# Attention layers of 16 heads worked four heads at a time, and a small attention layer run in another order

## The reference

```python
# causal (first): 16 heads of 8 channels, over the 256 positions of each sequence
scores = q @ k.T / sqrt(8) + triu(-1e8, k=1); out = softmax(scores) @ v; x += out @ Wo.T
# lead (fifth): 16 heads of 8 channels, over the LEADING axis: for each of the 256
# positions, the 8 sequences attend to one another (scores are 8 x 8 for each head)
scores = einsum('sbhd,tbhd->bhst', q, k) / sqrt(8); x += (softmax(scores) @ v) @ W.T
# binary (seventh): as causal without the mask, with weights mean|W| * sign(W) and biases
x += softmax(q @ k.T / sqrt(8)) @ v @ Wp.T + bp
```

## Time and profile before

| | us |
|---|---|
| median of 3 runs (4507.86 to 4510.74) | 4509.04 |
| the profiled execution, time | 4513.09 |
| its span, first to last instruction | 4511.3 |
| causal heads, first projection to last residual | 25.5 to 246.3 |
| lead, first projection to last residual | 3806.4 to 3921.0 |
| binary heads, first projection to last residual | 4104.3 to 4350.5 |
| TensorE busy, share of the span | 89% |

### The profile page before, as it was taken

The page is one execution under the profiler, slowest core; times in us unless marked ns, Lnnn a source line. Parts: engine busy times, 40 slices in busy tenths (PEclk is TensorE's granted clock), DMA queues, the critical chain, the costliest instruction groups (busy, mean ns, idle before and its releaser), DMA issues.

```text
span 4511.3 us, 169577 instructions
## 1 busy us (share of the span) xinstructions
PE 4027.8 (89%) x69543; PEld 2810.5 (62%) x69543; DVE 2763.2 (61%) x4602; ACT 2729.5 (61%) x5657; POOL 3001.0 (67%) x1858
## 2 busy tenths in 40 slices
PE   8979999999999999977999999999999995367975
PEld 5656666666666666635666666666666663154654
DVE  4556666666766667635667666676666663524541
ACT  5656676666766766635667667576675763134652
POOL 0068888888888888816888878788787882421011
PEclk9999999999999999989999999999999997587987
DMA  2023343434334343312334333343333330040004
GB/s 68 2 59 94 101 104 91 108 92 105 100 92 111 90 103 101 96 30 60 94 102 103 94 101 95 101 103 94 101 96 99 102 90 19 0 119 8 1 11 124
DMA packets 349841, 368.13 MB, mean 82 GB/s; under 512 B 58738, under 2 KB 285171, under 8 KB 348787
## 3 DMA queue, kind: packets, MB, share of 16 engines
q1 hardware_dynamic: 338834, 348.79, 30.0%
q0 software_dynamic: 2048, 4.20, 0.3%
q10 hardware_dynamic: 8160, 3.93, 0.3%
HBM read 246.99 MB, written 109.71 MB: 79 GB/s over the span
## 4 chain that ended last, share of the span: by engine, by line
PE 42%; ACT 2%; POOL 2%; DVE 2%; issue 2%; DMA 1%; DVEq 0%; POOLq 0%; ACTq 0%
PE banks L328 7%; PE banks L359 4%; PE banks L407 4%; PE banks L333 3%; PE banks L451 3%; PE banks L312 3%; PE banks L295 2%; PE banks L879 2%; PE banks L377 2%; PE banks L897 1%; PE banks L445 1%; PE banks L914 1%; PE banks L392 1%; PE banks L1345 1%; PE banks L1365 1%
## 5 line engine op out<-in xcount | busy, mean ns | idle before, releaser
L671 POOL TENSOR_TENSOR arena<-arena 128x512 f32<-128x512 f32 x768 | 960.0, 1271 | 461.3 <-DVE arena L600 266.5
L676 POOL TENSOR_TENSOR arena<-arena 128x1024 f32<-128x1024 f32 x384 | 905.9, 2359 | 30.1
L673 POOL TENSOR_TENSOR arena<-arena 128x1024 f32<-128x1024 f32 x384 | 908.1, 2365 | 0.0
L600 DVE SCALAR_TENSOR_TENSOR arena<-arena,banks 128x512 f32<-128x512 f32 x768 | 493.6, 684 | 537.3 <-ACT arena L500 528.7
L328 PE MATMUL banks<-w_qk,arena 128*128 128x512 f32 x1536 | 734.8, 601 | 16.0 <-DVE arena L700 10.6
L461 ACT COPY arena<-banks 128x512 f32<-128x512 f32 x384 | 224.6, 585 | 660.0 <-PE banks L407 660.0
L593 DVE TENSOR_REDUCE arena<-arena 128x8 f32<-128x512 f32 x768 | 494.0, 679 | 83.4 <-ACT arena L477 81.0
L477 ACT ACTIVATE arena<-banks 128x512 f32<-128x512 f32 x768 | 441.7, 594 | 62.0 <-PE banks L328 49.4
L407 PE MATMUL banks<-ident,arena 128*128 128x128 f32 x3072 | 427.1, 282 | 34.9 <-POOL arena L676 22.8
L328 PEld LDWEIGHTS banks<-w_qk,arena 128*128 128x128 f32 x1536 | 277.0, 193 | 272.1 <-issue 272.0
L333 PEld LDWEIGHTS banks<-w_v,arena 128*128 128x128 f32 x1536 | 293.9, 191 | 206.6 <-issue 186.5
(11 more groups left out here) (220 smaller groups left out, 6744.8 us busy)
## 6 DMA issues: line engine op xcount, KB each, us to landing
v_rows<-arena SPq DMA_DIRECT2D x1536, 64.0 KB
arena<-v_rows SPq DMA_DIRECT2D x768, 128.0 KB
arena<-v_rows SPq DMA_DIRECT2D x768, 112.0 KB
arena<-in_moe_w SPq DMA_DIRECT2D x30, 515.5 KB, 3.8
w_qk<-in_stack_qk SPq DMA_DIRECT2D x48, 256.0 KB, 3.0
w_v<-in_stack_v SPq DMA_DIRECT2D x48, 128.0 KB, 3.2
w_o<-in_stack_o SPq DMA_DIRECT2D x12, 512.0 KB
w_w<-in_stack_w SPq DMA_DIRECT2D x12, 341.0 KB, 3.0
```

The costliest lines, as they stand in the source:

```text
L600: last = nc.vector.scalar_tensor_tensor(qn[:, :, tile], rn, 1e12, bank(M, tile).rearrange("p (h q d) -> p h q d", h=GH, q=2), ALU.min, ALU ...
L671: nc.gpsimd.tensor_tensor(f.sined[:, :, :, half, :], x[:, :, :, 1 - half, :], sines[:, :, mine].unsqueeze(1).to_broadcast([D, GH, 4, DH // ...
L673: nc.gpsimd.tensor_tensor(rot, x.rearrange("p h t a d -> p h t (a d)"), cosines.unsqueeze(1).to_broadcast([D, GH, 4, DH]), ALU.mult).then_ ...
L676: nc.gpsimd.tensor_tensor(rot, rot, f.sined.rearrange("p h t a d -> p h t (a d)"), ALU.add).then_inc(S.rotated, 1)
```

## The change

Both head modules go by *quads*: 4 in each sequence, 32 steps, each quad being heads c, 4+c, 8+c and 12+c. The scores of the four heads go to banks 0 to 3, all at once, and the next quad's scores wait until all four heads have been exponentiated. DVE takes the maxima one head and one query tile at a time (8 instructions of 128 or 256 columns for a quad, in place of 2 of 1024) and signals after each head; ACT makes the exponentials of a head as soon as it has its maxima. Turning and copying goes in two halves of two heads. Causal scores and mask are placed so that 384 columns hold all that is computed (the mask covers 2 x 128 columns of each bank). The values of head c lie shifted by 8c rows in their 32, so the outputs of four quads accumulate in bank 6 in natural order: one Ln, Exp, multiply and one output matmul for a sequence, in place of four. TensorE's order in step n is: turn the first half of quad n-1, scores of quad n, outputs of quad n-2, turn the second half of quad n-1, projections. The last binarised weight is turned whole. In lead, buffers are doubled (four products), POOL makes all 16 query products, then all 16 value products; the softmax of t = 0 falls in the query products of t = 1.

```diff
 def pe_heads(M, pe, m):
+    def turn(h, half):
+        pe.wait_ge(S.probs, 2 * h.n + half + 1)
+        if h.n or half:
+            pe.wait_ge(S.copied_first, 2 * h.n + half)
+            pe.wait_ge(S.copied_second, 2 * h.n + half)
+        for i in range(2):
...
+                    last = pe.transpose(bank(M, 4 + i)[:, o:o + 128],
+                                        f.p[:, h.n % 2, 2 * half + i, qt, kt * 128:kt * 128 + 128], M.ident[:])
+        last.then_inc(S.turned, 1)
+    for n in range(QUADS + 3):
+        if 0 <= n - 1 < QUADS:
+            turn(Quad(m, n - 1), 0)
+        if n < QUADS:
+            if n >= 1:
+                pe.wait_ge(S.probs, 2 * n)
             if m.causal:
+                for j in range(4):
+                    pe.matmul(bank(M, j).rearrange("p (t k) -> p t k", t=2)[:, :, 0:128], M.identb[:],
+                              M.cmask[:, 0:2 * 128], start=True, stop=False, skip_group_check=True)
             for t in range(2):
+                for j in range(4):
                     r = slice(32 * j, 32 * j + 32)
+                    last = pe.matmul(bank(M, j)[:, cols], f.qm[r, h.b % 2, h.c, t * 128:t * 128 + 128],
+                                     f.k[r, h.b % 2, 0:cols.stop - cols.start], ...)
             last.then_inc(S.scores, 1)
+        if 0 <= n - 2 < QUADS:
+            h = Quad(m, n - 2)
+            pe.wait_ge(S.copied_first, 2 * h.n + 2)
+            pe.wait_ge(S.copied_second, 2 * h.n + 2)
+            ...  # 16 matmuls into bank 6, start only for c == 0, stop only for c == 3
+        if 0 <= n - 1 < QUADS:
+            turn(Quad(m, n - 1), 1)
+        if n % 4 == 0 and n // 4 + 1 < B:
+            project_qk(n // 4 + 1)
+        if n % 4 == 1 and n // 4 + 1 < B:
+            project_v(n // 4 + 1)
+        if n % 4 == 2 and n >= 6:
+            project_out(n // 4 - 1)
 def act_heads(M, act, m):      # dve_heads: the same order, with maxima in the place of exponentials
+    for n in range(QUADS + 3):
+        if 0 <= n - 1 < QUADS:
+            copy(Quad(m, n - 1), 0)
+        if n < QUADS:
+            exponentials(Quad(m, n), 0)
+        if 0 <= n - 1 < QUADS:
+            copy(Quad(m, n - 1), 1)
+        if n < QUADS:
+            exponentials(Quad(m, n), 1)
 def dve_heads(M, dve, m):
-    nc.vector.memset(f.v.rearrange("p a t h e -> p (a t h e)"), 0.0)
+    nc.vector.memset(f.vs.rearrange("p a g e -> p (a g e)"), 0.0)
+    def maxima(h, half):
+        dve.wait_ge(S.scores, h.n + 1)
+        for j in (2 * half, 2 * half + 1):
+            for t in range(2):
+                last = nc.vector.tensor_reduce(f.ntop[:, h.n % 2, j, t:t + 1], bank(M, j)[:, h.keys[t]], AX.X, ALU.max,
+                                               negate=True)
+            last.then_inc(S.maxed, 1)
 def pool_lead(M, pool, m):
+    for j in range(4 * B):
+        t, s = j // B % 2, j % B
+        if j >= 4:
+            if j - 4 < 2 * B:
+                pool.wait_ge(S.reduced, j - 3)
+            else:
+                pool.wait_ge(S.att, j - 3 - 2 * B)
+        if j < 2 * B:
+            ...  # product of query s with all keys of t
+        else:
+            pool.wait_ge(S.step, 4 * t + 4)
+            ...  # product of the probabilities of query s with all values of t
```

More of the change, by code:

```diff
@@ L957, in act_heads @@
     take_v(0)
[L958 to L984, removed]
-                                                bias=f.ntop[:, n % 2, 2 * i + t:2 * i + t + 1])
-            last.then_inc(S.probs, 1)
-            if h.x == 1 and h.b + 1 < B:
-                take_qk(h.b + 1)
-            if h.x == 3 and h.b + 1 < B:
-                take_v(h.b + 1)
@@ new lines, in copy, with exponentials @@
+    def copy(h, half):
+        act.wait_ge(S.turned, 2 * h.n + half + 1)
+        if h.n >= 2:
+            act.wait_ge(S.pv, h.n - 1)
+        nc.scalar.copy(f.pt[:, h.n % 2, 2 * half, 0:h.width], bank(M, 4, h.width)).then_inc(S.copied_first, 1)
+    def exponentials(h, half):
+        if h.n >= 2:
+            act.wait_ge(S.turned, 2 * h.n - 2)
+        for j in (2 * half, 2 * half + 1):
+            act.wait_ge(S.maxed, 4 * h.n + j + 1)
+            for t in range(2):
+                cols = h.keys[t]
+                last = nc.scalar.activation(f.p[:, h.n % 2, j, t, 0:cols.stop - cols.start], bank(M, j)[:, cols],
+                                            ACT.Exp, bias=f.ntop[:, h.n % 2, j, t:t + 1])
+        last.then_inc(S.probs, 1)
@@ new lines, in dve_heads @@
+    for n in range(QUADS + 3):
+        if 0 <= n - 1 < QUADS:
+            copy(Quad(m, n - 1), 0)
+        if n < QUADS:
+            maxima(Quad(m, n), 0)
+        if 0 <= n - 1 < QUADS:
+            copy(Quad(m, n - 1), 1)
+        if n < QUADS:
+            maxima(Quad(m, n), 1)
+        if n % 4 == 1 and n >= 5:
+            b = n // 4 - 1
+            dve.wait_ge(S.inverted, b + 1)
+            if b >= 1:
+                dve.wait_ge(S.out_projected, b)
+            nc.vector.tensor_tensor(f.ot, bank(M, 6)[:, 0:T], f.inv, ALU.mult).then_inc(S.divided, 1)
+        if n % 4 == 2 and n >= 6:
+            residual(n // 4 - 1)
@@ new lines, in pe_lead @@
+    for j in range(2 * B):
+        if j >= 4:
+            pe.wait_ge(S.qkv, j - 3)
+        o = j % B * T + j // B * 128
+        pe.matmul(bank(M, j % 4, 3 * D), M.z[:, o:o + 128], w.qkv, start=True, stop=True).then_inc(S.projected, 1)
+    for i in range(4):
+        t, half = i // 2, i % 2
+        pe.wait_ge(S.att, t * B + 4 * half + 4)
+        for s in range(4):
+            last = pe.transpose(bank(M, 4 + i % 2)[:, s * D:s * D + D], f.att[:, t, 4 * half + s, :], M.ident[:])
+        last.then_inc(S.turned, 1)
+        pe.wait_ge(S.at, i + 1)
+        if i >= 2:
+            pe.wait_ge(S.residual, i - 1)
+        pe.matmul(bank(M, 6 + i % 2), w.o, f.at, start=True, stop=True).then_inc(S.out_projected, 1)
@@ L1217, in dve_lead @@
+        nc.scalar.activation(pr, pr, ACT.Exp, scale=8.0 ** -0.5).then_inc(S.exped, 1)
+    for i in range(4):
+        act.wait_ge(S.turned, i + 1)
+        if i >= 1:
+            act.wait_ge(S.out_projected, i)
+        nc.scalar.copy(f.at, bank(M, 4 + i % 2)).then_inc(S.at, 1)
 def dve_lead(M, dve, m):
```

283 lines of the change are left out of this document (101 added, 182 removed).

## The result

The change makes the kernel slightly faster: a median of 4484.96 us (5 runs, 4472.51 to 4488.84) against 4509.04 (5 runs, 4506.81 to 4510.74), ratio 0.9943 with an interval of 0.9929 to 0.9958. That is 24.1 us less; the forecast was 27.9 less. The profiled spans are 4511.3 and 4483.1, 28.2 less.

A forecast was written before the change was run, and what follows sets the result against it. TensorE's order of work was taken to bound causal and binary, with neither POOL nor DVE full in lead. Terms -7.3 - 1.5 - 0.5 - 18.6 = -27.9 gave 4481.1 us against 4509.04; the 8-in-10 range was 4460 to 4510.

The forecast's parts named there:

- The bound moves from TensorE to the chain: Causal and binary: scores, outputs, turning, copy, maxima and exponentials in series set 6.3 and 7.1 us a quad.
- the first rival: Causal and binary: chain isn't met, TensorE still sets the pace; -103 in place of -9, about 4387 us; 3%.
- Maxima, four row groups: Heads: 256-column maxima take 0.42 us, 128-column ones 0.28; four row groups run together, 16 score instructions in about 1.1.
- The clock "taken as kept": TensorE in causal and binary: 20 to 30% idle doesn't cost the upper clock level by itself; nothing charged.
- the prediction's own signs: Wrong if score distances are off by 0.3 us or more, the clock falls, or lead's second softmax isn't covered.
- The rival that had this mechanism: Causal, binary: clock falls because TensorE waits; +3.5 us a quad, a quarter of quads giving +54, 4535; 8%.
- The start of binary: Clock at 0.50 until about 4131, so binary's first three quads take 26.1 us in all.
- The length of a sequence: Four quads take 25.2 us in causal against 26.12 before, and 28.4 in binary against 28.64.
- binary's account: Binary stage: 5.3 + 26.1 + 28 x 7.1 + 14.5 = 244.7 us against 246.2 before, -1.5.
- Lead: Lead: four buffers nearly cover the first softmax, POOL held about 1.6 us, DVE's sums set the pace later; -18.6 us.
- DVE full from its second softmax on: Sign in lead: DVE has no idle time from its second softmax, its end coming 19 us earlier.
- The sum: Whole kernel: causal -7.3, binary -1.5, last weight's transpose -0.5, lead -18.6, in all -27.9 us.

The follow-up runs named there:

- turn_first: The change with the second half of quad n-1 turned ahead of the outputs of quad n-2; 4411.63 us, ratio 0.9783.
- lead_old: The change's causal and binary heads with lead as before the change; 4513.82 us, ratio 0.9998.
- copy_late: The change with the second half's copy moved after the second maxima and exponentials on DVE and ACT; 4458.24 us, ratio 0.9884.
- short_after: The change with only causal, lead and binary kept, other modules left out; four executions: 622.27, 623.81, 635.32 and 635.45 us.
- short_fill_turn: short_after with eight more transposes, their output overwritten, ahead of the first half's turning; 622.24 us.
- short_fill_mm: short_after with two more matmuls of 256 columns, their output overwritten, ahead of the first half's turning; 622.69 us.
- short_before: The kernel before the change with only causal, lead and binary kept, other modules left out; 642.64 us.
- short_add_late: short_after with the second half turned ahead of the outputs, and lead's first two residuals added after the third sum of t = 1; 547.67 us.

## Why the prediction held, and where it did not, step by step

**The bound moves from TensorE to the chain: right.** The quads were to be 6.3 and 7.1; at full clock three of the four in a sequence take 6.35 in causal and two take 7.14 in binary, the others 6.44 to 6.72 and 7.23 to 7.34. Each link stands in the timeline, and cutting it in two places gave about what the links say. Without it the promised saving would have been taken at face value, as the first rival did. turn_first got a good part of that: 102 us less than before in the medians, of which some 16 are lead's.

**Maxima, four row groups: right.** 0.415 and 0.284 us; 16 score instructions in 1.08.

**The clock "taken as kept": this term was mis-sized.** By the prediction's own signs it is wrong if the clock falls, and the clock fell. The window at 1.00 with 4.10 of 6.00 busy, and the 28 of 40 in the same module after, show the level held while TensorE was 70% busy. They don't show that it always is. In these stages, at 77% to 81% busy with a wait of 1.0 to 1.4 us before most scores, the level fell to 0.50 for 3.4 us at a time, each costing 7.92 - 6.35 = 1.6 in causal (scores from 222.54 to 230.46) and 8.78 - 7.14 = 1.6 in binary. Two and four of them make some +10 in the profiled run, in a term that the sum had at nothing; lead_old had eight and four. The rival that had this mechanism expected whole stretches of quads at half speed, up to 3.5 a quad; what came was a small repeated tax. That it goes when the idle time is filled, or when the second half is turned first, is shown by the six profiles without a fall, one execution each. The busy share alone doesn't decide: copy_late had none in its steady causal part at 80%, short_after none in causal at 77%. Why one execution has two in causal and another eight, and why the single-head module has none in the stretch at 70%, stays open.

The Trainium skill, TensorE: Matmul & The Clock Gate (Part 4, PE-mode transpose), says that a transpose doesn't count as busy in the way a matmul does. By that rule the eight transposes of short_fill_turn should have left the low pieces in place; its profile has none in either steady part, as that of short_fill_mm, and the measurement decides.

**The start of binary: wrong in the other direction.** The first three quads took 6.9, 6.4 and 7.1 = 20.4, not 26.1: the clock rose 14 us after the first projection (at 4090.3), where it had needed 27 before (4131.6). The 5.7 was luck for the sum, since nothing in my working foresaw it. It is no accident of one execution, though: the five profiles of whole kernels with the new heads have 13.6 to 14.5, the two with the old 27.3 and 27.4. Nor does it belong to the new heads alone: in short_before the clock rose after 9.4, and its binary stage took 238.6 in place of 246.2, less than short_after's 245.3. No run isolates what sets it.

**The length of a sequence: a little short.** 25.5 and 25.8 by turns for 25.2, and 28.9 for 28.4. One quad in a sequence takes 6.44 or 6.72 in causal, and two take 7.23 and 7.34 in binary; in the quad shown the second exponentials begin 1.00 after their maxima in place of 0.71. Why, I haven't isolated. With 7 x 0.4 = 2.8 binary's account closes: 244.7 - 5.7 + 4 x 1.6 + 2.8 = 248.2, as measured. Causal: the first two quads took 5.99 + 5.24 = 11.2, not 13.4, and what follows the last scores 12.4, not 12.8; the other 29 quads add 2.8 and the two falls 3.2. 213.6 - 2.2 - 0.4 + 2.8 + 3.2 = 217.0, as measured.

**Lead: right, 97.4 for 96.0.** POOL starts 8.9 after the first projection, not 7.8. It is held 2.29, not 1.6 and not "under 2": the softmax of t = 0 runs beside POOL now, and its subtraction takes 2.50 where it took 1.23 before, with POOL idle. The product that POOL began meanwhile (3829.89) took 3.33 in place of 2.34, so the sixteen take 37.9, not 36.9. The subtraction before, and the product after:

```profile
3835.82 1.23 DVE L1230 TENSOR_TENSOR arena<-arena 128x1024 f32<-128x1024 f32 x1
```

```profile
3829.89 3.33 POOL L1288 TENSOR_TENSOR arena<-arena 128x1024 f32<-128x1024 f32 x1
```

The second softmax takes 8.9 from the last reduction, not 8.4. Against these 1.1 + 0.7 + 1.0 + 0.5 = 3.3 us, the sums take 14.55 and 14.47 for eight, not 15.4. "DVE full from its second softmax on" was right but for the wait of 3.4 that short_add_late then removed.

**The sum.** In the stages -3.8, +2.0 and -17.2 make -19.0 for -27.4. Ahead of binary's stage 2.1 were gained, where the sum had 0.5 for the one transpose, and ahead of causal's and lead's 1.6 were lost. The rest was made good by the stacks and the second mixture in this one pair of profiles. The short kernels give the cleaner account: 642.64 to 622.27 and 623.81 is some -20, and in the profiles the cut of the table gives lead -19.7 (126.9 to 107.2), causal -6.2 (237.0 to 230.8) and binary, with its store and two falls, +7.3 (267.9 to 275.2). So the heads' part is worth about nothing here, and less when the clock falls more often: lead_old's causal was 8.3 longer than the change's.

## What to carry to other kernels

When work is merged to unload a full engine, write out the chain that the new order makes (who must wait for whom before the same buffer is used again) and sum it beside the engine's own work: the longer sets the pace, and an order of instructions within a step can be worth more than the merge (here 35.4 + 44.1 = 79.5 us in the two stages for two moved lines). TensorE may also lose its clock now and then when its idle time is spread through a stage. Check a small gain module by module, and with the untouched modules cut away, before believing that its size was understood.

## What the hardware did that I had not expected

- The granted TensorE clock fell to 0.50 (the 1.2 GHz level) for single pieces of 3.4 us, in stages that were 77% to 81% busy; in turn_first's steady parts at 92% and 96% none came, nor in those of the filled kernels at 91% and 92%. In lead_old the falls came once a sequence, 27.3 us apart.
- With eight transposes more for each quad the level stayed up in both steady parts, as with two matmuls more.
- A subtraction of two operands in SBUF of 1024 columns on DVE took 1.23 us with POOL idle (before), and 2.50 and 1.74 with POOL's products beside it; the product that POOL began meanwhile took 3.33 in place of 2.34, and 2.95 in place of 1.96. That is 1.3 and 0.5 more on DVE, and 1.0 more on POOL each time.
